# Message stage of a two-layer graph network in pairs of supersteps: half as many VectorE and ACT instructions, each twice as long

## The chip, the cores and the metric

The kernel runs on one core of one Trainium2 chip. The metric is the device time of one execution in microseconds (us), as the median of several runs.

## The reference, cut to what matters

18750 nodes with 64 features, 318750 edges, two layers. Each layer computes a gate for every edge, a degree normalisation per node, and then a message for every edge that is summed at the edge's row node:

```python
mask = jnp.clip(gate * (ZETA - GAMMA) + GAMMA, 0.0, 1.0)[:, 0]
rowsum = jax.ops.segment_sum(mask, row, num_segments=N_NODES) + EPS_DEG
d_inv_sqrt = jnp.clip(rowsum ** (-0.5), 0.0, 10.0)
vals = mask * d_inv_sqrt[row] * d_inv_sqrt[col]
msg = vals[:, None] * f2                      # f2 = x[col]
return jax.ops.segment_sum(msg, row, num_segments=N_NODES)
```

The kernel multiplies x by d_inv_sqrt first (y), so that a message is mask * y[col]; the factor of the row is applied after the sum.

## The kernel before, in words

The edges are sorted once by their column and cut into T = 156 supersteps of 2048 edges (128 lanes by CT = 16). In each layer L the stages follow one another: node scores, masks, y, **messages**, sums over rows (buckets). The change touches the message stage alone. Engines run their own instruction streams in program order and wait for one another through semaphores; a helper, steps, runs a body once, then in a hardware loop, then once more.

For superstep t the message stage does this:

- SP loads 2048 column numbers, relative to a window of 128 nodes, to all 128 partitions (crelp_d to half of the tile bcast, 512 KB, "index load") and the window's 128 rows of y, split into three bf16 parts (y_window).
- VectorE compares the index tile with the partition number: one-hots of 128 x 2048 in bf16 (col_hots, L1281).
- TensorE multiplies 16 blocks of one-hots by the three parts, 48 matmuls (spread_y, L1633). The 16 x 64 f32 values per lane take two of the six PSUM banks of psG; superstep t uses the pair of banks t % 2.
- VectorE multiplies them by the mask (scale, L1286) into scaled. ACT rounds that to bf16 (first_bf16, L835; it also writes a column of lane numbers, L836), VectorE subtracts (first_rest, L1291), ACT rounds the rest (second_bf16, L840), and VectorE subtracts again (last_part, L1295): three bf16 parts that add up to the f32 value. They stand in staged, which has four slots; superstep t uses slot t % 4.
- ACT issues the store of the slot to msg_d in DRAM (store_messages, L844, 776 KB).

The order is written out by hand. VectorE runs scale(t), last_part(t-1), one-hots(t+2), first_rest(t). ACT runs first_bf16(t), the store of t-1, second_bf16(t). SP runs the index load of t and the y window of t; the index load waits until one-hots(t-2) are made, which free its half of bcast. Each use of a staged slot begins with a wait in first_bf16 for the store that used the slot before:

```python
act.wait_ge(scaled_ready, L * T + t + 1)
wait(act, messages_stored[u], (L * T // 4 + i) * 16)
act.activation(staged[:, u, :, 0:D], scaled[:, u % 2, :, :], ACT.Copy).then_inc(first_part, 1)
```

Of the kernel before, what the change touches and what calls it, by code (L numbers as in the profile page):

```python
# [9 lines left out]
CH = 8  # L10
# [47 lines left out]
def build(nc, x, src, dst, noise, params, out):  # L58
# [21 lines left out]
    with ctx:  # L80
# [3 lines left out]
        def sem(name):  # L84
            return ctx.enter_context(nc.semaphore(name))
# [33 lines left out]
        psG = ctx.enter_context(nc.psum_tensor("psG", [P, 6, 512], f32))  # L119
        psR = ctx.enter_context(nc.psum_tensor("psR", [P, 2, 512], f32))  # L120
# [107 lines left out]
        col_one_hots = scratch[:, 0:2 * ST // 2].bitcast(bf16).rearrange("p (h e) -> p h e", h=2)  # L228
        scaled = flat_merge[:, 0:2 * CT * D].rearrange("p (h j d) -> p h j d", h=2, j=CT)
# [45 lines left out]
        lo_loaded, crel_loaded, msg_index_loaded, y_window_loaded = ([sem(f"{n}{h}") for h in range(2)] for n in ("lo_loaded", "crel_loaded", "msg_index_loaded", "y_window_loaded"))  # L275
# [59 lines left out]
        def _(sp):  # L335
# [91 lines left out]
            for L in range(2):  # L427
# [46 lines left out]
                def load_superstep(i):  # L474
                    for h in range(2):
                        t = i * 2 + h
                        wait(sp, col_hots_ready, L * T + t - 1)
                        sp.dma_start(bcast[:, 2 * h:2 * h + 2, :].rearrange("p a e -> p (a e)"),
                                     spread(crelp_d, t)).then_inc(msg_index_loaded[h], 16)
                        wait(sp, y_taken, L * T + t - 1)  # L480
                        sp.dma_start(y_window[:, h, :], y3_d[L][bass.ds(window(t * 2), P), :]).then_inc(y_window_loaded[h], 16)
                with sp.If(is_local):
                    sp.wait_ge(one_hot_ready[0], (L + 1) * T)
                    sp.wait_ge(mask_turn_kept, TURNS * (L + 1))
                    blocks = mask_d[0:whole].rearrange("(g c l) -> c g l", c=P, l=P)
# [15 lines left out]
                    steps(sp, 0, T // 2, load_superstep)  # L501
# [126 lines left out]
        def _(act):  # L628
# [70 lines left out]
            for L in range(2):  # L699
# [131 lines left out]
                def first_bf16(i, u):  # L831
                    t = i * 4 + u
                    act.wait_ge(scaled_ready, L * T + t + 1)
                    wait(act, messages_stored[u], (L * T // 4 + i) * 16)
                    act.activation(staged[:, u, :, 0:D], scaled[:, u % 2, :, :], ACT.Copy).then_inc(first_part, 1)  # L835
                    act.activation(staged[:, u, :, MW:MW + 1].bitcast(u16), row_lane[:, bass.ds(t * CT, CT)].unsqueeze(2), ACT.Copy)  # L836

                def second_bf16(t, u):
                    act.wait_ge(rest_ready, L * T + t + 1)
                    act.activation(staged[:, u, :, D:2 * D], scaled[:, u % 2, :, :], ACT.Copy).then_inc(second_part, 1)  # L840

                def store_messages(t, u):
                    act.wait_ge(third_part, L * T + t + 1)
                    act.dma_start(msg_d[bass.ds(t * TR, ST), :].rearrange("(l j) w -> l (j w)", j=CT),  # L844
                                  staged[:, u, :, :].rearrange("p j w -> p (j w)")).then_inc(messages_stored[u], 16)

                def body_local(i):
                    for u in range(4):
                        t = i * 4 + u
                        first_bf16(i, u)  # L850
                        if u > 0 or not isinstance(i, int) or i > 0:
                            store_messages(t - 1, (u - 1) % 4)
                        second_bf16(t, u)
                with act.If(is_local):
                    act.wait_ge(row_lane_loaded, 16)
                    steps(act, 0, T // 4, body_local)
                    store_messages(T - 1, 3)
                    if L == 0:
                        steps(act, 0, NG, node_beside)
# [21 lines left out]
        def _(dve):  # L881
# [240 lines left out]
            for L in range(2):  # L1122
# [154 lines left out]
                def col_hots(i, h):  # L1277
                    t = i * 2 + h
                    dve.wait_ge(msg_index_loaded[h], (L * T // 2 + i + 1) * 16)
                    wait(dve, y_taken, L * T + t - 1)  # L1280
                    dve.tensor_scalar(col_one_hots[:, h, :], bcast[:, 2 * h:2 * h + 2, :].rearrange("p a e -> p (a e)"), pid[:, 0:1], None, ALU.is_equal).then_inc(col_hots_ready, 1)  # L1281

                def scale(t, h):
                    dve.wait_ge(y_taken, L * T + t + 1)
                    wait(dve, third_part, L * T + t - 1)
                    dve.tensor_tensor(scaled[:, h, :, :], psG[:, 2 * h:2 * h + 2, :].rearrange("p a (j d) -> p (a j) d", d=D),  # L1286
                                      ga[:, bass.ds(t * CT, CT)].unsqueeze(2).to_broadcast([P, CT, D]), ALU.mult).then_inc(scaled_ready, 1)

                def first_rest(t, u):
                    dve.wait_ge(first_part, L * T + t + 1)  # L1290
                    dve.tensor_tensor(scaled[:, u % 2, :, :], scaled[:, u % 2, :, :], staged[:, u, :, 0:D], ALU.subtract).then_inc(rest_ready, 1)  # L1291

                def last_part(t, u):
                    dve.wait_ge(second_part, L * T + t + 1)
                    dve.tensor_tensor(staged[:, u, :, 2 * D:MW], scaled[:, u % 2, :, :], staged[:, u, :, D:2 * D], ALU.subtract).then_inc(third_part, 1)  # L1295

                def messages_local(i):
                    last = isinstance(i, int) and i == T // 4 - 1
                    for u in range(4):
                        t = i * 4 + u  # L1300
                        scale(t, u % 2)
                        if u > 0 or not isinstance(i, int) or i > 0:
                            last_part(t - 1, (u - 1) % 4)
                        if not last or u < 2:
                            col_hots(i * 2 + u // 2 + 1, u % 2)
                        first_rest(t, u)
# [32 lines left out]
                with dve.If(is_local):  # L1339
# [5 lines left out]
                    for h in range(2):  # L1345
                        col_hots(0, h)
                    dve.wait_ge(mask_loaded, 16 * (L + 1))
                    steps(dve, 0, T // 4, messages_local)
                    last_part(T - 1, 3)
# [71 lines left out]
        def _(pe):  # L1421
# [79 lines left out]
            for L in range(2):  # L1501
# [123 lines left out]
                def spread_y(i):  # L1625
                    for h in range(2):
                        t = i * 2 + h
                        pe.wait_ge(col_hots_ready, L * T + t + 1)
                        pe.wait_ge(y_window_loaded[h], (L * T // 2 + i + 1) * 16)
                        wait(pe, scaled_ready, L * T + t - 1)  # L1630
                        for k in range(CT):
                            for m in range(3):
                                ins = pe.matmul(psG[:, 2 * h + k // CH, k % CH * D:(k % CH + 1) * D], col_one_hots[:, h, k * P:(k + 1) * P],  # L1633
                                                y_window[:, h, m * D:(m + 1) * D], start=m == 0, stop=m == 2)
                        ins.then_inc(y_taken, 1)
# [46 lines left out]
                with pe.If(is_local):  # L1682
                    steps(pe, 0, T // 2, spread_y)
                    pe.wait_ge(scaled_ready, (L + 1) * T)
# [27 lines left out]
```

## Time and profile before

| | us |
|---|---|
| median of 3 runs | 5665.64 |
| lowest and highest | 5664.9 and 5666.88 |
| the profiled execution, its own time | 5668.84 |
| span of the profiled execution | 5667.1 |
| message stage of layer 0, first scale to last last_part | 2614.6 to 3262.2 |

The span runs from the first instruction of the program to the last; the execution's own time holds a little more around it. Views give times from the span's start. The message stage comes twice, once per layer, 156 supersteps each.

### The profile page before, as it was taken

The page shows a single profiled execution, that of the slowest core. Times are in us where ns is not written, and L with a number is a line of the kernel's source. Part 1 is how long each engine was busy: PE and PEld are TensorE (multiplying, and loading weights), DVE is VectorE, ACT ScalarE, POOL GpSimd, SP SyncE. Part 2 cuts the span into 40 slices and gives each one's busy share as a digit, 9 for nine tenths or more (in the row PEclk, how much of TensorE's full clock was granted, in tenths as well). Part 3 has the DMA queues.
Part 4 walks back from the last instruction along what each step waited for, and adds up shares of the span by engine and source line. Part 5 has one row for each costly group of instructions (what it writes and reads, how often), then busy time and mean ns, then how long its engine had stood idle before and what let it go on. Part 6 is the DMA issues. An engine that isn't in the chain of part 4 may idle for free. (4 is left out here: it accounts for less than half of the span.)

```text
span 5667.1 us, 162410 instructions
## 1 busy us (share of the span) xinstructions
PE 3982.8 (70%) x56036; PEld 3597.1 (63%) x56036; DVE 5132.4 (91%) x10844; ACT 2508.2 (44%) x5126; POOL 1165.2 (21%) x1562
## 2 busy tenths in 40 slices
PE   2777777777587888873555579978888445554777
PEld 2666666666455888872544468868888344443776
DVE  8999999999953999988999989979999799998888
ACT  2666666666423555542555511145555245554000
POOL 0000000000000333330000067723333100000776
PEclk6776777777655555556677789965555577777999
DMA  3000000000132777657999989967766589997999
GB/s 76 0 0 0 0 0 0 0 0 0 16 9 107 230 233 234 232 167 242 329 330 331 322 321 379 376 227 232 233 230 231 147 294 328 331 330 278 385 382 347
DMA packets 428684, 1120.70 MB, mean 198 GB/s; under 512 B 206962, under 2 KB 212707, under 8 KB 428023
## 3 DMA queue, kind: packets, MB, share of 16 engines
q1 hardware_dynamic: 316700, 549.97, 31.6%
q0 software_dynamic: 65856, 316.89, 14.7%
q10 hardware_dynamic: 46036, 252.74, 11.6%
q8 instruction: 42, 0.69, 0.1%
q14 instruction: 50, 0.41, 0.0%
HBM read 873.65 MB, written 279.36 MB: 203 GB/s over the span
## 5 line engine op out<-in xcount | busy, mean ns | idle before, releaser
L1633 PE MATMUL psG<-y_window,area 128*128 128x64 bf16 x14976 | 672.9, 217 | 777.8 <-DVE area L1281 619.8
L1633 PEld LDWEIGHTS psG<-y_window,area 128*128 128x128 bf16 x14976 | 629.2, 115 | 821.7 <-issue 502.3
L644 ACT ACTIVATE work<-iota,work 128x149 bf16<-128x149 f32 x2496 | 789.0, 406 | 0.0
L1452 PE MATMUL psG<-area,work 128*128 128x112 bf16 x2496 | 550.8, 390 | 336.0 <-DVE area L1004 336.0
L588 POOL DMA_INDIRECT work<-msg_d,widx x396 | 428.5, 1082 | 1657.9 <-issue 1634.8
L1452 PEld LDWEIGHTS psG<-area,work 128*128 128x128 bf16 x2496 | 357.2, 148 | 484.4 <-issue 338.5
L1445 PE MATMUL psG<-work,merge 128*128 128x148 bf16 x4992 | 548.2, 295 | 67.1 <-ACT work L644 67.1
L1445 PEld LDWEIGHTS psG<-work,merge 128*128 128x128 bf16 x4992 | 531.4, 132 | 89.9 <-issue 65.6
L840 ACT ACTIVATE work<-merge 128x1024 bf16<-128x1024 f32 x312 | 330.1, 1058 | 549.6 <-DVE merge L1291 549.6
L1666 PE MATMUL psG<-work,edge 128*128 128x192 bf16 x4752 | 443.6, 249 | 142.8 <-DVE edge L1316 141.2
L773 ACT ACTIVATE edge<-merge,npid 128x2048 bf16<-128x2048 uint16 x156 | 312.4, 2003 | 488.0 <-DMA merge<-crel_d 478.3
L1666 PEld LDWEIGHTS psG<-work,edge 128*128 128x128 bf16 x4752 | 412.4, 145 | 176.4 <-DVE edge L1316 101.1
L1316 DVE TENSOR_TENSOR edge<-y_edge,ids 128x1024 bf16<-128x1024 int16 x738 | 467.5, 688 | 8.7
L835 ACT ACTIVATE work<-merge 128x1024 bf16<-128x1024 f32 x312 | 330.1, 1058 | 198.5 <-issue 94.1
L990 DVE SCALAR_TENSOR_TENSOR work<-merge,work,psG 128x148 bf16<-128x148 f32 x1248 | 367.6, 366 | 38.8 <-ACT work L635 38.8
L990 DVE SCALAR_TENSOR_TENSOR area<-merge,work,psG 128x148 bf16<-128x148 f32 x1248 | 367.6, 366 | 23.9 <-DVE work L985 18.2
L1295 DVE TENSOR_TENSOR work<-merge,work 128x1024 bf16<-128x1024 f32 x312 | 382.4, 1226 | 2.2 <-ACT work L840 2.2
L1286 DVE TENSOR_TENSOR merge<-psG,edge 128x1024 f32<-128x1024 f32 x312 | 380.1, 1218 | 2.4 <-PE psG L1633 2.4
L1291 DVE TENSOR_TENSOR merge<-merge,work 128x1024 f32<-128x1024 f32 x312 | 380.4, 1219 | 1.0 <-ACT work L835 1.0
L547 POOL PARTITION_ALL_REDUCE wide<-wide x1 | 1.8, 1750 | 1534.5 <-DVEq L1059 1534.5
L775 ACT ACTIVATE edge<-edge 128x2048 bf16<-128x2048 bf16 x156 | 299.0, 1916 | 5.0
L565 POOL TENSOR_SCALAR area<-area 128x32 f32<-128x32 f32 x156 | 63.6, 407 | 1120.6 <-ACT area L789 1120.6
(274 smaller groups left out, 8092.8 us busy)
## 6 DMA issues: line engine op xcount, KB each, us to landing
msg_d<-work ACTq DMA_DIRECT2D x312, 776.0 KB, 4.7
area<-rlo_d SPq DMA_DIRECT2D x312, 512.0 KB, 4.2
merge<-crel_d SPq DMA_DIRECT2D x312, 512.0 KB, 5.0
area<-crelp_d SPq DMA_DIRECT2D x312, 512.0 KB, 5.8
y_window<-y_d SPq DMA_DIRECT2D x312, 48.0 KB, 3.8
y_d<-cur SPq DMA_DIRECT2D x7, 1008.0 KB, 3.8
y_d<-work SPq DMA_DIRECT2D x7, 1008.0 KB, 4.7
work<-msg_d,widx POOLq DMA_INDIRECT x396, 6.9
```

The source lines that it names most:

```text
L588: pool.indirect_dma_start(out=windows[par][:, rows.start:rows.stop, :].rearrange("p s w -> p (s w)"), out_offset=None, in_=msg_d, in_offse ...
L644: ins = act.activation(below[:, h, k, :], iota_all[:, :], ACT.Sign, bias=keyf[:, bass.ds(t * CT + k, 1)], scale=-1.0)
L835: act.activation(staged[:, u, :, 0:D], scaled[:, u % 2, :, :], ACT.Copy).then_inc(first_part, 1)
L990: ins = dve.scalar_tensor_tensor(picks[h][:, k, :], iota_half, keyf[:, bass.ds(t * CT + k, 1)], psG[:, h, 0:HB], ALU.is_equal, ALU.mult, a ...
L1286: dve.tensor_tensor(scaled[:, h, :, :], psG[:, 2 * h:2 * h + 2, :].rearrange("p a (j d) -> p (a j) d", d=D), ga[:, bass.ds(t * CT, CT)].un ...
L1291: dve.tensor_tensor(scaled[:, u % 2, :, :], scaled[:, u % 2, :, :], staged[:, u, :, 0:D], ALU.subtract).then_inc(rest_ready, 1)
L1295: dve.tensor_tensor(staged[:, u, :, 2 * D:MW], scaled[:, u % 2, :, :], staged[:, u, :, D:2 * D], ALU.subtract).then_inc(third_part, 1)
L1316: dve.tensor_tensor(q_one_hots[s][:, g, :, :], iota_rows, ids[:, s, g * WIN:(g + 1) * WIN].unsqueeze(1).to_broadcast([P, P, WIN]), ALU.is_ ...
L1445: ins = pe.matmul(psG[:, h, 0:HB], sides[:, s, :], below[:, h, k, s:s + HB], start=s == 0 and k == 0, stop=s == 1 and k == CT - 1)
L1452: ins = pe.matmul(psG[:, 2 + h, 0:RECS * CT], place[:, h, :, k], spread_rec[:, h, :, :, k], start=k == 0, stop=k == CT - 1)
L1633: ins = pe.matmul(psG[:, 2 * h + k // CH, k % CH * D:(k % CH + 1) * D], col_one_hots[:, h, k * P:(k + 1) * P], y_window[:, h, m * D:(m + 1 ...
L1666: ins = pe.matmul(psG[:, slot_, 0:MW], q_one_hots[slot_][:, r // WIN, :, r % WIN], windows[slot_][:, r, 0:MW], start=r == 0, stop=r == WG ...
```

## The change

The stage works on pairs of supersteps, n = 0 to 77 per layer. One VectorE or ACT instruction does a step for both supersteps of a pair, on 2048 f32 values per lane instead of 1024 (4096 one-hots instead of 2048). A pair takes four PSUM banks; since two pairs alternate, psG and psR become views of one PSUM tensor ps of eight banks, and the stage uses all of them. There are two sets of one-hots (scratch and a piece of edge), two sets of scaled (merge and a piece of edge) and four y windows. bcast and staged keep their size: bcast now holds one pair, staged two pairs. The order on each engine is that of before with pairs in the place of supersteps; one-hots are made two pairs ahead.

```diff
-        y_window = sb("y_window", [P, 2, MW], bf16)
+        y_window = sb("y_window", [P, 4, MW], bf16)
...
-                def load_superstep(i):
-                    for h in range(2):
-                        t = i * 2 + h
-                        wait(sp, col_hots_ready, L * T + t - 1)
-                        sp.dma_start(bcast[:, 2 * h:2 * h + 2, :].rearrange("p a e -> p (a e)"),
-                                     spread(crelp_d, t)).then_inc(msg_index_loaded[h], 16)
-                        wait(sp, y_taken, L * T + t - 1)
-                        sp.dma_start(y_window[:, h, :], y3_d[L][bass.ds(window(t * 2), P), :]).then_inc(y_window_loaded[h], 16)
+                def load_pairs(i):
+                    for v in range(2):
+                        n = i * 2 + v
+                        wait(sp, col_hots_ready, L * TP + n)
+                        for h in range(2):
+                            sp.dma_start(bcast[:, 2 * h:2 * h + 2, :].rearrange("p a e -> p (a e)"),
+                                         spread(crelp_d, n * 2 + h)).then_inc(msg_index_loaded[h], 16)
+                        wait(sp, y_taken, L * TP + n - 1)
+                        for h in range(2):
+                            sp.dma_start(y_window[:, 2 * v + h, :], y3_d[L][bass.ds(window(n * 4 + 2 * h), P), :]).then_inc(y_window_loaded[v], 16)
...
-                    wait(act, messages_stored[u], (L * T // 4 + i) * 16)
-                    act.activation(staged[:, u, :, 0:D], scaled[:, u % 2, :, :], ACT.Copy).then_inc(first_part, 1)
...
+                    for u in range(2 * v, 2 * v + 2):
+                        wait(act, messages_stored[u], (L * T // 4 + i) * 16)
+                    act.activation(staged[:, 2 * v:2 * v + 2, :, 0:D], scaled[v], ACT.Copy).then_inc(first_part, 1)
...
+                def store_messages(n, v):
+                    act.wait_ge(third_part, L * TP + n + 1)
+                    for h in range(2):
+                        act.dma_start(msg_d[bass.ds((n * 2 + h) * TR, ST), :].rearrange("(l j) w -> l (j w)", j=CT),
+                                      staged[:, 2 * v + h, :, :].rearrange("p j w -> p (j w)")).then_inc(messages_stored[2 * v + h], 16)
...
+                def body_local(i):
+                    for v in range(2):
+                        n = i * 2 + v
+                        first_bf16(i, v)
+                        if v > 0 or not isinstance(i, int) or i > 0:
+                            store_messages(n - 1, 1 - v)
+                        second_bf16(n, v)
...
+                def col_hots(n, v):
+                    for h in range(2):
+                        dve.wait_ge(msg_index_loaded[h], (L * TP + n + 1) * 16)
+                    wait(dve, y_taken, L * TP + n - 1)
+                    dve.tensor_scalar(col_one_hots[v].rearrange("p h e -> p (h e)"), bcast[:, :, :].rearrange("p a e -> p (a e)"), pid[:, 0:1], None, ALU.is_equal).then_inc(col_hots_ready, 1)
...
+                        scale(n, v)
+                        if v > 0 or not isinstance(i, int) or i > 0:
+                            last_part(n - 1, 1 - v)
+                        if not last:
+                            col_hots(n + 2, v)
+                        first_rest(n, v)
...
+                        wait(pe, scaled_ready, L * TP + n - 1)
+                        for h in range(2):
+                            for k in range(CT):
+                                for m in range(3):
+                                    ins = pe.matmul(ps[:, 4 * v + 2 * h + k // CH, k % CH * D:(k % CH + 1) * D], col_one_hots[v][:, h, k * P:(k + 1) * P],
+                                                    y_window[:, 2 * v + h, m * D:(m + 1) * D], start=m == 0, stop=m == 2)
```

On ACT, in the hardware loop of the message stage, one superstep of before (merge is the tile that holds scaled, work holds staged, edge the lane numbers; messages_stored0 to 3 tell of the landing of the stores of the four slots):

```order
L835 ACTIVATE work<-merge 128x16x64 [waits messages_stored0]
L836 ISA
L836 ACTIVATE work<-edge 128x16
L844 ISA [waits third_part]
L844 DMA msg_d<-work 128x3104
L840 ACTIVATE work<-merge 128x16x64 [waits rest_ready]
```

and one pair of the changed kernel at the same place:

```order
L840 ACTIVATE work<-merge 128x32x64 [waits messages_stored1,messages_stored0]
L841 ISA
L841 ACTIVATE work<-edge 128x32
L850 ISA [waits third_part]
L850 DMA msg_d<-work 128x3104
L850 ISA
L850 DMA msg_d<-work 128x3104
L845 ACTIVATE work<-merge 128x32x64 [waits rest_ready]
```

The first copy now waits for two stores, and two stores are issued behind one another. The next pair uses slots 2 and 3, the one after it slots 0 and 1 again.

On SP, in the hardware loop of the message stage, one superstep of before (area is the tile that holds bcast; TENSOR_LOAD reads the window's first node):

```order
L478 ISA [waits col_hots_ready]
L478 DMA area<-crelp_d 128x2048
L421 ISA [waits y_taken]
L421 TENSOR_LOAD bases
L421 ISA x2
L481 ISA
L481 DMA y_window<-y_d 128x192
```

and one pair of the changed kernel:

```order
L481 ISA [waits col_hots_ready]
L481 DMA area<-crelp_d 128x2048
L481 ISA
L481 DMA area<-crelp_d 128x2048
L313 REGISTER_ALU
L423 ISA [waits y_taken]
L423 TENSOR_LOAD bases
L423 ISA x2
L485 ISA
L485 DMA y_window<-y_d 128x192
```

Both index loads stand behind one wait for the one-hots of the pair before; the second y window of the pair follows with a TENSOR_LOAD of its own.

## Rows read from the trace of the kernel before

**Rows 1.** The page's head: busy time, share of the span and instructions by engine.
```profile
PE 3982.8 (70%) x56036; PEld 3597.1 (63%) x56036; DVE 5132.4 (91%) x10844; ACT 2508.2 (44%) x5126; POOL 1165.2 (21%) x1562
```

**Rows 2.** Stretch: busy PE, PEld, DVE, ACT, POOL (instructions), PEclk, DMA share, GB/s.
```profile
2900.00:3000.00 100.00, 51.91 (x1158) 48.50 (x1155) 100.00 (x98) 54.79 (x73) 0.00 (x0) 0.71 0.94 331
```

**Rows 3.** Groups of instructions, 2600 to 3320 us: busy, mean ns | idle before, releaser.
```profile
L1295 DVE TENSOR_TENSOR work<-merge,work 128x1024 bf16<-128x1024 f32 x156 | 191.2, 1226 | 1.1 <-ACT work L840 1.1
L1291 DVE TENSOR_TENSOR merge<-merge,work 128x1024 f32<-128x1024 f32 x156 | 190.2, 1219 | 0.5 <-ACT work L835 0.5
L1286 DVE TENSOR_TENSOR merge<-psG,edge 128x1024 f32<-128x1024 f32 x156 | 190.1, 1219 | 1.2 <-PE psG L1633 1.2
L1281 DVE TENSOR_SCALAR area<-area,pid 128x2048 bf16<-128x2048 uint16 x156 | 116.6, 748 | 4.6 <-DMA area<-crelp_d 4.6
```

**Rows 4.** Timeline of one superstep: start, duration, engine (q: sequencer), line, what.
```profile
2903.35 2.74 PE L1633 MATMUL psG<-y_window,area 128*128 128x64 bf16 x48 [2.09 <-DVE area L1281]
2903.48 0.33 SPq L478 DMA_DIRECT2D area<-crelp_d  x1
2904.35 1.22 DVE L1286 TENSOR_TENSOR merge<-psG,edge 128x1024 f32<-128x1024 f32 x1
2904.46 1.06 ACT L840 ACTIVATE work<-merge 128x1024 bf16<-128x1024 f32 x1 [1.79 <-DVE merge L1291]
2905.55 1.23 DVE L1295 TENSOR_TENSOR work<-merge,work 128x1024 bf16<-128x1024 f32 x1
2905.60 1.06 ACT L835 ACTIVATE work<-merge 128x1024 bf16<-128x1024 f32 x1
...
2906.70 0.75 DVE L1281 TENSOR_SCALAR area<-area,pid 128x2048 bf16<-128x2048 uint16 x1
...
2906.95 0.35 ACTq L844 DMA_DIRECT2D msg_d<-work  x1
2907.36 1.22 DVE L1291 TENSOR_TENSOR merge<-merge,work 128x1024 f32<-128x1024 f32 x1
...
2908.49 1.22 DVE L1286 TENSOR_TENSOR merge<-psG,edge 128x1024 f32<-128x1024 f32 x1
```

**Rows 5.** VectorE, line L946, a longer f32 operation: busy, mean ns.
```profile
L946 DVE TENSOR_TENSOR work<-edge 128x2496 f32<-128x2496 f32 x1 | 2.8, 2759 | 0.0
```

**Rows 6.** ACT, line L775, an instruction of 2048 elements: busy, mean ns.
```profile
L775 ACT ACTIVATE edge<-edge 128x2048 bf16<-128x2048 bf16 x156 | 299.0, 1916 | 5.0
```

**Rows 7.** What ended the idle time before L835, 2620 to 3280 us.
```profile
  DVE merge L1286: 5.9, 37
```

**Rows 8.** The store, line L844, 2620 to 3280 us: issue to landing.
```profile
DMA to landing us min/median/max: 3.3/4.8/6.5
```

**Rows 9.** The index load, line L478, 2620 to 3280 us: issue to landing.
```profile
DMA to landing us min/median/max: 5.1/5.9/7.0
```

**Rows 10.** DMA queues, 2904.6 to 2905.9 us: packets, MB, share (q10: stores; q1: SP's loads).
```profile
q10 hardware_dynamic: 82, 0.51, 98.3%
q1 hardware_dynamic: 31, 0.01, 3.5%
```

**Rows 11.** DMA queues, 2907.0 to 2908.0 us: packets, MB, share.
```profile
q1 hardware_dynamic: 89, 0.35, 91.7%
q10 hardware_dynamic: 1, 0.00, 0.1%
```

**Rows 12.** Timeline of the stage's first and last microseconds in layer 0.
```profile
2607.04 0.34 SPq L478 DMA_DIRECT2D area<-crelp_d  x1
...
2610.91 0.75 DVE L1281 TENSOR_SCALAR area<-area,pid 128x2048 bf16<-128x2048 uint16 x1 [3.66 <-DMA area<-crelp_d]
...
2614.57 1.22 DVE L1286 TENSOR_TENSOR merge<-psG,edge 128x1024 f32<-128x1024 f32 x1 [1.21 <-PE psG L1633]
...
3262.23 0.34 ACTq L844 DMA_DIRECT2D msg_d<-work  x1
3267.60 7.90 DVE L1352 MEMSET work<- 128x9408 f32 x1 [5.41 <-issue]
```

More of the change, by code:

```diff
@@ L118, in build @@
         dtmp = sb("dtmp", [P, CH], f32)
-        psG = ctx.enter_context(nc.psum_tensor("psG", [P, 6, 512], f32))
-        psR = ctx.enter_context(nc.psum_tensor("psR", [P, 2, 512], f32))
+        ps = ctx.enter_context(nc.psum_tensor("ps", [P, 8, 512], f32))
+        psG, psR = ps[:, 0:6, :], ps[:, 6:8, :]
         b_out = sb("b_out", [P, HI, 3], bf16)
         b_window = sb("b_window", [P, 4, 4], bf16)
-        y_window = sb("y_window", [P, 2, MW], bf16)
+        y_window = sb("y_window", [P, 4, MW], bf16)
         bases = sb("bases", [1, NS], i32)
@@ L227, in build @@
         msg = work[:, 0:4 * CH * D].rearrange("p (u k d) -> p u k d", u=4, k=CH)
-        col_one_hots = scratch[:, 0:2 * ST // 2].bitcast(bf16).rearrange("p (h e) -> p h e", h=2)
-        scaled = flat_merge[:, 0:2 * CT * D].rearrange("p (h j d) -> p h j d", h=2, j=CT)
+        col_one_hots = [t.rearrange("p (h e) -> p h e", h=2) for t in (scratch[:, 0:ST].bitcast(bf16), far[:, 0:2 * ST])]
+        scaled = [t.rearrange("p (h j d) -> p h j d", h=2, j=CT) for t in (flat_merge[:, 0:2 * CT * D], far[:, 2 * ST:4 * ST].bitcast(f32))]
         staged = work[:, 0:2 * CT * MR].bitcast(bf16).rearrange("p (h j w) -> p h j w", h=4, j=CT)
@@ L274, in build @@
         span_ready, widest_ready, local_ready, b_ready, b_stored = (sem(n) for n in ("span_ready", "widest_ready", "local_ready", "b_ready", "b_stored"))
-        lo_loaded, crel_loaded, msg_index_loaded, y_window_loaded = ([sem(f"{n}{h}") for h in range(2)] for n in ("lo_loaded", "crel_loaded", "msg_index_loaded", "y_window_loaded"))
+        lo_loaded, crel_loaded, msg_index_loaded = ([sem(f"{n}{h}") for h in range(2)] for n in ("lo_loaded", "crel_loaded", "msg_index_loaded"))
+        y_window_loaded = [sem(f"y_window_loaded{v}") for v in range(2)]
         b_window_loaded = [sem(f"b_window_loaded{s}") for s in range(4)]
@@ L838, in second_bf16 @@
[L838 to L845, printed above, removed]
@@ L847, in body_local, with first_bf16 @@
-                def body_local(i):
[L848 to L853, printed above, removed]
+                def first_bf16(i, v):
+                    n = i * 2 + v
+                    act.wait_ge(scaled_ready, L * TP + n + 1)
+                    for u in range(2 * v, 2 * v + 2):
+                        wait(act, messages_stored[u], (L * T // 4 + i) * 16)
+                    act.activation(staged[:, 2 * v:2 * v + 2, :, 0:D], scaled[v], ACT.Copy).then_inc(first_part, 1)
+                    act.activation(staged[:, 2 * v:2 * v + 2, :, MW:MW + 1].bitcast(u16), row_lane[:, bass.ds(n * 2 * CT, 2 * CT)].rearrange("l (u j) -> l u j", u=2).unsqueeze(3), ACT.Copy)
@@ new lines, in second_bf16 @@
+                def second_bf16(n, v):
+                    act.wait_ge(rest_ready, L * TP + n + 1)
+                    act.activation(staged[:, 2 * v:2 * v + 2, :, D:2 * D], scaled[v], ACT.Copy).then_inc(second_part, 1)
+                def store_messages(n, v):
[3 more added lines that the diff above has]
+                                      staged[:, 2 * v + h, :, :].rearrange("p j w -> p (j w)")).then_inc(messages_stored[2 * v + h], 16)
@@ L1283, in scale @@
[L1283 to L1291, printed above, removed]
@@ new lines, in scale, with first_rest @@
+                def scale(n, v):
+                    dve.wait_ge(y_taken, L * TP + n + 1)
+                    wait(dve, third_part, L * TP + n - 1)
+                    dve.tensor_tensor(scaled[v].rearrange("p h j d -> p (h j) d"), ps[:, 4 * v:4 * v + 4, :].rearrange("p a (j d) -> p (a j) d", d=D),
+                                      ga[:, bass.ds(n * 2 * CT, 2 * CT)].unsqueeze(2).to_broadcast([P, 2 * CT, D]), ALU.mult).then_inc(scaled_ready, 1)
+                def first_rest(n, v):
+                    dve.wait_ge(first_part, L * TP + n + 1)
+                    dve.tensor_tensor(scaled[v], scaled[v], staged[:, 2 * v:2 * v + 2, :, 0:D], ALU.subtract).then_inc(rest_ready, 1)
@@ L1297, in messages_local, with last_part @@
+                def last_part(n, v):
+                    dve.wait_ge(second_part, L * TP + n + 1)
+                    dve.tensor_tensor(staged[:, 2 * v:2 * v + 2, :, 2 * D:MW], scaled[v], staged[:, 2 * v:2 * v + 2, :, D:2 * D], ALU.subtract).then_inc(third_part, 1)
                 def messages_local(i):
                     last = isinstance(i, int) and i == T // 4 - 1
[L1299 to L1306, printed above, removed]
+                    for v in range(2):
+                        n = i * 2 + v
+                        scale(n, v)
[4 more added lines that the diff above has]
+                        first_rest(n, v)
@@ L1344, in _ @@
                     dve.memset(staged[:, :, :, MW:MR], 0.0)
-                    for h in range(2):
-                        col_hots(0, h)
+                    for v in range(2):
+                        col_hots(v, v)
                     dve.wait_ge(mask_loaded, 16 * (L + 1))
                     steps(dve, 0, T // 4, messages_local)
-                    last_part(T - 1, 3)
+                    last_part(TP - 1, 1)
                     for u in range(4):
@@ L1625, in spread_y @@
                 def spread_y(i):
[L1626 to L1634, printed above, removed]
+                    for v in range(2):
+                        n = i * 2 + v
+                        pe.wait_ge(col_hots_ready, L * TP + n + 1)
+                        pe.wait_ge(y_window_loaded[v], (L * TP + n - v + 2) * 16)
+                        wait(pe, scaled_ready, L * TP + n - 1)
[4 more added lines that the diff above has]
+                                                    y_window[:, 2 * v + h, m * D:(m + 1) * D], start=m == 0, stop=m == 2)
                         ins.then_inc(y_taken, 1)
```

21 lines of the change are left out of this document (5 added, 16 removed).

## The prediction, as it was written before the result

> **What bounds the kernel now.** I went from the whole to the stage, then to one superstep, then to its transfers. The page's head shows VectorE as the busiest engine, 91% of the span [rows 1]. That is an average over stages, so the next view is a stretch inside the stage that changes: from 2900 to 3000 us VectorE is busy for all of the 100 us, TensorE for half, ACT for 55, and the DMA engines have a share of 0.94 at 331 GB/s [rows 2]. Two things are full there, and the question is which gives way. The groups say VectorE: over a layer's stage its four operations have hardly 5 us of idle time ahead of any of them [rows 3]. The timeline shows the period: scale starts at 2904.35 and the next at 2908.49, 4.14 us for a superstep and 8.28 for two [rows 4]. Both layers have 312 supersteps, 156 pairs, 1292 us or 23% of the span. So a pair of the changed kernel that takes 0.1 us more or less than 8.28 moves the kernel by 15.6 us, and 0.2% of the kernel, about what a measurement can tell from no change, is 11.3 us.
>
> The transfers have room in time but not much in rate. A store lands 4.8 us after its issue (3.3 to 6.5) [rows 8], an index load 5.9 us after (5.1 to 7.0) [rows 9]. The store's slot is next written four supersteps later, three periods or 12 us after its issue, and in fact ACT's first copy is never held by a store, only 5.9 us in all by VectorE [rows 7]. The index load that is issued at 2903.48 is needed two supersteps after the one-hots that released it, about 7.4 us later; it lands with 1.5 us to spare.
>
> **What the change does on VectorE.** An f32 operation of 1024 elements lasts 1219 ns, one of 2496 lasts 2759 [rows 3, 5]: 1.046 ns an element, so 2048 last 1219 + 1024 x 1.046 = 2.29 us. On the engine an operation takes up its start-to-start time, which is 0.08 less: 1.14 of 1.22 us where nothing is awaited (last_part at 2905.55 to 2906.70 is 1.15, first_rest at 2907.36 to 2908.49 is 1.13) [rows 4]. Three of them take 3 x 2.21 = 6.63 us. The one-hots take 0.66 us (2906.70 to 2907.36); no row shows 4096 of them, at most they double to 1.32, at least the fixed 0.08 is saved and a little more, 1.2; I take 1.25. VectorE then needs 7.88 us for a pair instead of 8.28: 0.40 less, 62 us over 156 pairs. That is all that can be won, and only if nothing else becomes late.
>
> The Trainium skill, "VectorE: DVE Perf Modes", section on the TRN2 errata, says that an instruction with SBUF sources pays a fixed extra latency, once for a large tile and once for each of many small ones, and gives 58 cycles at 0.96 GHz; by that, four instructions fewer per pair are worth an estimated 0.24 us, 38 us in all. The rows above say 0.40, and the sum uses them.
>
> **What it does to the stores.** This is the term that I think decides. staged keeps four slots, and a pair takes two. Pair n's first copy writes the slots of pair n-2, whose stores ACT has issued just one period earlier, behind the first copy of pair n-1. The program order on ACT is thus a loop of one period: first copy, lane column, two stores issued, both landed, first copy. Its length is the time from the issue of the first store to the landing of the second, call it D, and then ACT's own part. The first copy of 2048 elements lasts about 1.9 us (an ACT instruction of 2048 shows 1916 ns [rows 6]); from a first copy to the store's issue there are now 1.35 us for a copy of 1.06, so 0.29 more [rows 4]; with 0.1 for the wake-up the part is 2.3 us. A pair can't be shorter than D + 2.3. To get the 7.88 of VectorE, D must be 5.6 us or less; to equal 8.28, 6.0.
>
> What is D? The first store alone has 3.3 us at best and 4.8 as a median [rows 8]. The second stands behind it on the same DMA engines: 0.51 MB passed in 1.3 us while stores ran [rows 10], 392 GB/s, so its 776 KB (0.795 MB) add 2.0 us: D is 5.3 to 6.8 with nothing between. Now the order of the transfers. In the stretch from 2904.6 to 2905.9 the store queue moves 0.51 MB and SP's queue 0.01 MB in 31 small packets, although the index load had been issued at 2903.48; from 2907.0 to 2908.0, when the store is through, SP's queue moves 0.35 MB and the store queue one packet [rows 4, 10, 11]. So the engines don't mix two transfers; they finish one and turn to the other queue. In the changed kernel the two stores and the two index loads are issued in the same part of each period. If the queues take turns, an index load goes between the two stores: 524 KB at 350 GB/s [rows 11], 1.5 us more. D is then 6.8 to 8.3, and the pair 9.1 to 10.6 us. I take 9.5, nearer the lower end, since the median of 4.8 already has a part of an index load ahead of the store and would count it twice.
>
> The Trainium skill, "DMA: Bandwidth & Descriptors", section Queues, rings and completion order, says that each DMA engine goes round robin between the queue rows that have work, a whole packet at a time. The trace agrees that transfers go in blocks; no stretch here has two transfers waiting on both queues, so it doesn't show the turn itself. By the rule the index load goes between the stores (9.5 us a pair), without it behind both (the second case below).
>
> **What it does to the index loads.** bcast held two supersteps, each half loaded again while the other waited; now both halves belong to one pair, and the loads for a pair are issued when the one-hots of the pair before are made. They have one period less the one-hots, 7.88 - 1.25 - 0.2 (issue) = 6.4 us, for 1 MB. With no store about, the first load of the stage is issued at 2607.04 and its one-hots start at 2610.91: 3.9 us [rows 12]. The second load of a pair adds 1.5: 5.4. That leaves 1.0 us for what stores take, and one store takes 2.0. So this loop stalls the one-hots too; at 9.5 us a pair it has 8.05, which fits 5.4 + 2.0.
>
> **What hides.** TensorE needs 2.74 us at its slower rate for a superstep [rows 4], 5.5 for a pair; it starts when one-hots two pairs ahead are made and has more than a period. The second y window comes later by one more read on SP, and TensorE's lead covers it; without that lead each late y window would cost its own microsecond.
>
> **Ends of the stage.** VectorE makes the one-hots of two pairs ahead of the first scale, now in two rounds: 2607.0 + 5.4 + 1.3 + 0.2 + 5.4 + 1.3 puts that scale at 2620.6, 6.0 us after the 2614.57 of before [rows 12]. At the end VectorE waits 5.4 us for the last store, issued at 3262.23 [rows 12]; a second store adds 2.0, the longer last copy and subtraction 0.8 + 1.1. About 10 us a layer, 20 in all.
>
> **The sum.** 156 x (9.5 - 8.28) = 190 us, and 20 for the ends: 210 more. The profiled execution took 5668.84 us, 1.7 above its span and 3.2 above the median of the runs; on the median, 5665.6 + 210 gives 5876 us.
>
> **Rivals.**
> 1. Turns as above, chance 0.55: pair 9.1 to 10.2 us, 5814 to 5986, likeliest 5876.
> 2. Both stores go first, in order of issue, 0.22. D is 5.3 to 6.8, the store loop 7.6 to 9.1. The index loads land after both stores: first issue 4.7 us into the period (scale and last_part are 4.42, then ACT), 5.3 + 3.0 later at best, at 13.0, while the one-hots want them at 7.88 + 4.42 = 12.3. A stall w moves the need twice (period and place), so w = 0.35 at best, and 1.1 with 4.8 for the first store: 8.2 to 9.1, middle 8.5. That is 156 x 0.22 + 20 = 54 more, 5720; at its lower end, 8.2, the stage itself gains 12 us and the ends cost 20: 5674, which can't be told from no change.
> 3. The other side, faster, 0.16: the transfers stay hidden. The place is ACT's first copy; it decides at D = 5.6 us. For it speaks that the fastest store took 3.3 us, and 3.3 + 2.0 = 5.3 would do, if the index loads keep out of the way; against it that the share of 0.94 leaves no stretch without a transfer ahead. Then 62 us are won and 20 paid: 5624.
> 4. Worse than turns, 0.07: both stores and both loads in one chain with the median store, 10.6 us: 156 x 2.32 + 20 = 382, 6048.
>
> Chances: faster 0.16 (case 3), within 0.2% 0.07 (the low end of case 2), slower 0.77. The range from 5615 to 5990 leaves out half of case 3 and case 4 with the edge of case 1, 0.16 together. Case 1's own range is 5814 to 5986.
>
> **What would show it.** Right: ACT's first copy waits for a store's landing in nearly each pair, VectorE's first_rest waits for that copy, and the VectorE share in the stage falls from all to about 0.83; the store's median landing rises above 6 us for the second of a pair; VectorE's f32 operations show 2.29 us and the one-hots about 1.35. A period near 7.9 with no waits at the first copy is case 3; waits only at the one-hots, for index loads, are case 2. Wrong as a whole would be a copy of 2048 elements that takes much more than 1.9 us on ACT, or a DMA that mixes the queues by the row.

## The result and the profile after

The changed kernel takes 5754.31 us (median of 4 runs, 5747.99 to 5767.25) against 5665.6, 89 us more; the ratio is estimated at 1.0159, with a 95% interval from 1.0147 to 1.0171. It is slower, as forecast, but by 89 us and not by 210. The traced execution is the longest of the four, 5767.25 us, 98.4 more than the traced one of before; what is read from its trace adds up to that, not to the 89.

The page's head of the changed kernel, which answers to [rows 1], and the two lines of its chain of work that ended last:

```profile
PE 4051.6 (70%) x56036; PEld 3689.7 (64%) x56036; DVE 5066.1 (88%) x10220; ACT 2429.8 (42%) x4658; POOL 1165.4 (20%) x1562
...
DMA 10%; DVE 6%; issue 3%; POOL 1%; SPq 1%; PE 0%; DVEq 0%; ACT 0%; POOLq 0%; ACTq 0%
DMA area<-crelp_d 8%; DVE edge L1322 2%; DVE area L1287 1%; POOL work L592 1%; DVE edge L1287 1%; DMA area<-msg_d,widx 1%; DMA work<-msg_d,widx 1%; SPq L481 1%; POOL area L592 0%; PE ps L1673 0%; DVE merge L1322 0%; DVE summed L1328 0%; DVE
```

VectorE is busy for 66 us less and the span is 98 us longer. The chain of work that ended last goes through the index loads, area<-crelp_d, with 8% of the span. The stretch that answers to [rows 2] (busy PE, PEld, DVE, ACT, POOL, then PEclk, DMA share, GB/s):

```profile
2900.00:3000.00 100.00, 54.47 (x1077) 52.90 (x1074) 89.33 (x46) 46.65 (x36) 0.00 (x0) 0.69 0.91 310
```

VectorE now idles for 11 of 100 us, and the DMA engines move less than before. The timeline of two pairs, which answers to [rows 4] (L1287 one-hots, L1292 scale, L1297 first_rest, L1301 last_part, L840 first copy, L845 second copy):

```profile
2904.80 1.29 DVE L1287 TENSOR_SCALAR edge<-area,pid 128x4096 bf16<-128x4096 uint16 x1 [2.16 <-issue]
2906.01 2.28 DVE L1297 TENSOR_TENSOR edge<-edge,work 128x2048 f32<-128x2048 f32 x1
...
2906.27 0.86 SPq L481 DMA_DIRECT2D area<-crelp_d  x2
...
2908.21 2.28 DVE L1292 TENSOR_TENSOR merge<-ps,edge 128x2048 f32<-128x2048 f32 x1
...
2910.41 2.28 DVE L1301 TENSOR_TENSOR work<-edge,work 128x2048 bf16<-128x2048 f32 x1
2910.66 1.91 ACT L840 ACTIVATE work<-merge 128x2048 bf16<-128x2048 f32 x1 [0.42 <-DVE merge L1292]
...
2912.87 0.86 ACTq L850 DMA_DIRECT2D msg_d<-work  x2
2913.10 1.29 DVE L1287 TENSOR_SCALAR area<-area,pid 128x4096 bf16<-128x4096 uint16 x1 [0.41 <-issue]
...
2914.56 1.64 SPq L481 DMA_DIRECT2D area<-crelp_d  x2
...
2919.07 1.91 ACT L840 ACTIVATE work<-edge 128x2048 bf16<-128x2048 f32 x1 [0.54 <-DMA msg_d<-work]
...
2922.28 1.29 DVE L1287 TENSOR_SCALAR edge<-area,pid 128x4096 bf16<-128x4096 uint16 x1 [1.29 <-issue]
```

Read it from one set of one-hots to the next. They end at 2906.09, their index loads are issued at 2906.27, and the next one-hots begin at 2913.10, 6.8 us later; those release loads at 2914.56, and the ones after begin at 2922.28, 7.7 us later. VectorE has a gap ahead of each ("issue": the view doesn't name a landing here). From the issues and landings in the trace, 2700 to 3200 us, the second load of a pair lands 7.2 us after the first one's issue (median; 5.8 to 9.0), and the one-hots start 0.08 us after that landing in 52 of 57 pairs. The first copy on ACT is held by a store once in this stretch: the stores are issued at 2912.87 and the copy starts at 2919.07. The waits from 2700 to 3200 us (total, times, longest) say the same:

```profile
DVE edge L1287 <- issue: 37.3, 26, 2.7
DVE area L1287 <- issue: 20.0, 20, 2.2
ACT work L840 <- DMA msg_d<-work: 15.3, 17, 1.1
```

In these 500 us, 56 pairs, VectorE loses 57 us at the one-hots, 1.0 us a pair, and ACT 15 us at the first copy. What ACT waits there hardly reaches VectorE: before first_rest, which needs the first copy, its groups from 2600 to 3400 us show 0.7 us, the other set of scaled 0.0:

```profile
L1297 DVE TENSOR_TENSOR edge<-edge,work 128x2048 f32<-128x2048 f32 x39 | 89.1, 2285 | 0.7 <-ACT work L840 0.7
L1297 DVE TENSOR_TENSOR merge<-merge,work 128x2048 f32<-128x2048 f32 x39 | 89.1, 2284 | 0.0
```

The mean period is 8.855 us in layer 0 and 8.708 in layer 1: 77 periods of each against 8.28 make 77 us. The stage as a whole, from the first index load to the clearing of work behind it, grew by 53.6 and 43.4 us, so 20 of these 97 us belong to its ends.

Where do the index loads spend 7 us? The DMA queues from 2914.4 to 2917.0 us and from 2919.0 to 2920.2 (packets, MB, share), which answer to [rows 10, 11]:

```profile
q10 hardware_dynamic: 185, 1.05, 104.8%
...
q1 hardware_dynamic: 110, 0.42, 96.7%
```

In the first stretch the two stores pass, 1.05 of their 1.59 MB in 185 packets, and not one packet of SP's queue, though its loads are issued at 2914.56. The index loads come after the second store, not after the first.

### The profile page after: what moved, and what is told of

Its sections match the earlier page's. It is cut to its first block and busy times, and to the rows that moved or that the text cites. A ratio compares the mean times of both kernels' runs of the same rounds, so it can differ in the third digit from the quotient of the medians.

```text
span 5765.4 us, 159492 instructions
## 1 busy us (share of the span) xinstructions
PE 4051.6 (70%) x56036; PEld 3689.7 (64%) x56036; DVE 5066.1 (88%) x10220; ACT 2429.8 (42%) x4658; POOL 1165.4 (20%) x1562
## 5 line engine op out<-in xcount | busy, mean ns | idle before, releaser
L1458 PE MATMUL ps<-area,work 128*128 128x112 bf16 x2496 | 551.0, 390 | 338.5 <-DVE area L1010 338.5
L1640 PE MATMUL ps<-y_window,area 128*128 128x64 bf16 x7488 | 379.9, 233 | 482.8 <-DVE area L1287 481.3
L1640 PEld LDWEIGHTS ps<-y_window,area 128*128 128x128 bf16 x7488 | 369.7, 126 | 493.0 <-issue 315.9
L1451 PE MATMUL ps<-work,merge 128*128 128x148 bf16 x4992 | 543.6, 293 | 69.9 <-ACT work L648 69.9
L1451 PEld LDWEIGHTS ps<-work,merge 128*128 128x128 bf16 x4992 | 526.7, 131 | 92.7 <-issue 66.6
L1640 PE MATMUL ps<-y_window,edge 128*128 128x64 bf16 x7488 | 366.2, 229 | 298.5 <-DVE edge L1287 298.5
L1673 PE MATMUL ps<-work,edge 128*128 128x192 bf16 x4752 | 444.4, 250 | 161.2 <-DVE edge L1322 159.7
L1673 PEld LDWEIGHTS ps<-work,edge 128*128 128x128 bf16 x4752 | 413.0, 145 | 195.0 <-DVE edge L1322 102.2
L996 DVE SCALAR_TENSOR_TENSOR work<-merge,work,ps 128x148 bf16<-128x148 f32 x1248 | 367.2, 362 | 39.6 <-ACT work L639 39.6
L996 DVE SCALAR_TENSOR_TENSOR area<-merge,work,ps 128x148 bf16<-128x148 f32 x1248 | 367.3, 362 | 23.9 <-DVE work L991 18.2
L845 ACT ACTIVATE work<-edge 128x2048 bf16<-128x2048 f32 x78 | 149.2, 1913 | 333.2 <-DVE edge L1297 333.2
L845 ACT ACTIVATE work<-merge 128x2048 bf16<-128x2048 f32 x78 | 149.2, 1913 | 309.7 <-DVE merge L1297 309.7
```

The source lines that it names most:

```text
L845: act.activation(staged[:, 2 * v:2 * v + 2, :, D:2 * D], scaled[v], ACT.Copy).then_inc(second_part, 1)
L996: ins = dve.scalar_tensor_tensor(picks[h][:, k, :], iota_half, keyf[:, bass.ds(t * CT + k, 1)], psG[:, h, 0:HB], ALU.is_equal, ALU.mult, a ...
L1451: ins = pe.matmul(psG[:, h, 0:HB], sides[:, s, :], below[:, h, k, s:s + HB], start=s == 0 and k == 0, stop=s == 1 and k == CT - 1)
L1458: ins = pe.matmul(psG[:, 2 + h, 0:RECS * CT], place[:, h, :, k], spread_rec[:, h, :, :, k], start=k == 0, stop=k == CT - 1)
L1640: ins = pe.matmul(ps[:, 4 * v + 2 * h + k // CH, k % CH * D:(k % CH + 1) * D], col_one_hots[v][:, h, k * P:(k + 1) * P], y_window[:, 2 * v ...
L1673: ins = pe.matmul(psG[:, slot_, 0:MW], q_one_hots[slot_][:, r // WIN, :, r % WIN], windows[slot_][:, r, 0:MW], start=r == 0, stop=r == WG ...
```

## The experiments

Two loops are told apart below. The index loop is: one-hots, the two index loads that they release, both landed, next one-hots. The store loop is the one that goes through the landing of a pair's two stores and the first copy that waits for it. D is, as in the prediction, the time from the issue of a pair's first store to the landing of its second; where no window is named, it is the median from 2700 to 3200 us.

**A second index buffer.** The loads of pair n wait for the one-hots of pair n-2; the buffer lies in a free part of edge.

```diff
+        index = [bcast[:, :, :].rearrange("p a e -> p (a e)"), far[:, 4 * ST:6 * ST].bitcast(u16)]
...
-                        wait(sp, col_hots_ready, L * TP + n)
+                        wait(sp, col_hots_ready, L * TP + n - 1)
...
-                            sp.dma_start(bcast[:, 2 * h:2 * h + 2, :].rearrange("p a e -> p (a e)"),
-                                         spread(crelp_d, n * 2 + h)).then_inc(msg_index_loaded[h], 16)
+                            sp.dma_start(index[v][:, h * ST:(h + 1) * ST],
+                                         spread(crelp_d, n * 2 + h)).then_inc(msg_index_loaded[v], 16)
...
-                    dve.tensor_scalar(col_one_hots[v].rearrange("p h e -> p (h e)"), bcast[:, :, :].rearrange("p a e -> p (a e)"), pid[:, 0:1], None, ALU.is_equal).then_inc(col_hots_ready, 1)
+                    dve.tensor_scalar(col_one_hots[v].rearrange("p h e -> p (h e)"), index[v], pid[:, 0:1], None, ALU.is_equal).then_inc(col_hots_ready, 1)
```

> The changed kernel with a second buffer for the indices of a pair, so that the index loads of pair n wait for the one-hots of pair n-2 instead of n-1. Index theory (the one-hots, the two index loads they release and the next one-hots form a loop of one period; second landing 7.2 us after the first issue plus 1.5 us makes the 8.9 us a pair): the loop has two periods now, the next bound is the store loop (second store lands 6.0 us after the first issue, plus 2.2) at 8.2 to 8.3 us a pair, 156 x 0.6 = about 95 us less, 5660 us. Store theory (the loop of first copy, stores and first copy sets the period, the waits at the one-hots only follow): no change, 5754 us within 10. Full engines (the 16 DMA engines are nearly always busy, and any wait that goes comes back elsewhere): about 8.6 us a pair, 5710 us.

Measured: 5767.72 us (median of 4 runs that lie far apart, 5672.66 to 5860.95), a ratio of 1.0179 to before (1.013 to 1.0228). Against the changed kernel the four lie from 82 us less to 107 more, so whether this edit alone helps isn't decided. The trace is of the 5672.66 us run, with 8.19 and 8.24 us a pair. In it the waits at the one-hots are gone, and from 2700 to 3200 us the first copy has this one:

```profile
ACT work L841 <- DMA msg_d<-work: 116.6, 61, 2.9
```

Every pair waits for a store now; VectorE loses 22 of these 500 us. D is 7.4 us (median), not 6.0. In the traced run one loop went and the other took its place, at the 8.2 us a pair that I had expected; but that agreement is luck, since I had added 2.2 to a D of 6.0, and 7.4 + 2.2 would be 9.6. The other three runs, 5744 to 5861 us, weren't traced, and what makes them longer is open.

**Six staged slots.** The first copy of pair n waits for the stores of pair n-3; the loops of ACT and VectorE take six pairs a turn.

```diff
-        staged = work[:, 0:2 * CT * MR].bitcast(bf16).rearrange("p (h j w) -> p h j w", h=4, j=CT)
+        staged = work[:, 0:3 * CT * MR].bitcast(bf16).rearrange("p (h j w) -> p h j w", h=6, j=CT)
...
-                        wait(act, messages_stored[u], (L * T // 4 + i) * 16)
+                        wait(act, messages_stored[u], (L * TP // 3 + i * 2 + p // 3) * 16)
...
```

> The changed kernel with six staged slots instead of four, so that the first copy of pair n waits for the stores of pair n-3 instead of n-2. Index theory: no change, 5754 us within 10, the first copy's 22 us of waits for stores go and the waits at the one-hots take their place. Store theory: the loop has two periods, the pair falls to the 8.2 us or less that VectorE and the index loads leave, about 5650 us. Full engines: no change.

Measured: 5756.27 us (5756.13 to 5765.61), ratio 1.0159 (1.0142 to 1.0176): no change from the changed kernel. The first copy's waits for stores are gone, and the one-hots still wait, from 2700 to 3200 us:

```profile
DVE area L1288 <- issue: 31.7, 28, 2.0
DVE edge L1288 <- issue: 18.6, 23, 1.6
```

So the store loop, on which my prediction stood, doesn't set the period of the changed kernel.

**Both.** The two edits together.

> The changed kernel with the second index buffer and with six slots. If the two loops are the whole cause: VectorE's own 8.0 us a pair (3 x 2.2 + 1.3 to 1.4), 156 x 0.9 = 140 us less than the changed kernel, about 5615 us, and faster than the kernel before by the 40 to 50 us. Full engines: 8.3 us a pair as in the kernel before, about 5670 us, with VectorE still waiting.

Measured: 5601.36 us (5599.3 to 5603.4), ratio 0.9884 (0.9868 to 0.9901). It beats the changed kernel by 153 us and the kernel before by 65. The stretch from 2700 to 2900 us:

```profile
2700.00:2900.00 200.00, 118.46 (x2496) 115.02 (x2496) 200.00 (x103) 103.92 (x77) 0.00 (x0) 0.72 0.99 351
```

VectorE is full again, and so are the DMA engines, 0.99 at 351 GB/s. A pair takes 7.77 us. With six slots in both, the second index buffer is worth 155 us (5756.27 to 5601.36): the index loop set the period. The landings of single transfers are no shorter, stores first, index loads second (issue to landing, min, median, max):

```profile
DMA to landing us min/median/max: 3.4/5.6/8.6
...
DMA to landing us min/median/max: 4.3/7.4/9.1
```

They are longer than the medians of 4.8 and 5.9 in [rows 8, 9]; two periods of slack hide them.

**One-hots in two halves**, each waiting for its own index load and releasing it.

```diff
-                        wait(sp, col_hots_ready, L * TP + n)
                         for h in range(2):
+                            wait(sp, col_hots_ready, L * T + n * 2 + h - 1)
...
                     for h in range(2):
                         dve.wait_ge(msg_index_loaded[h], (L * TP + n + 1) * 16)
-                    wait(dve, y_taken, L * TP + n - 1)
-                    dve.tensor_scalar(col_one_hots[v].rearrange("p h e -> p (h e)"), bcast[:, :, :].rearrange("p a e -> p (a e)"), pid[:, 0:1], None, ALU.is_equal).then_inc(col_hots_ready, 1)
+                        wait(dve, y_taken, L * TP + n - 1)
+                        dve.tensor_scalar(col_one_hots[v][:, h, :], bcast[:, 2 * h:2 * h + 2, :].rearrange("p a e -> p (a e)"), pid[:, 0:1], None, ALU.is_equal).then_inc(col_hots_ready, 1)
...
```

> The changed kernel with the one-hots of a pair made by two instructions, each of which waits for its own half of the indices and releases it. Index theory: the first half's load is issued 0.7 us earlier and its one-hots need the first landing (6.0 us) and not the second (7.2), so the loop shortens by 0.6 to 1.0 us to about 8.1 us a pair, VectorE pays 0.07 to 0.1; 5650 to 5680 us. Store theory and full engines: the 0.1 us a pair is lost or nothing changes, 5754 to 5770 us.

Measured: 5774.1 us (5758.26 to 5787.47), ratio 1.0198 (1.0181 to 1.0215). My expectation missed. The loads go out closer behind the stores, the first one 1.1 us after the first store and not 2.2 (medians): they land 7.7 and 8.9 us after the first load's issue, and D is 7.4. The first copies and the one-hots both wait, but VectorE loses its 45 us at the one-hots alone, so it is still the index loop, at 8.77 us a pair. From 2700 to 3200 us:

```profile
ACT work L840 <- DMA msg_d<-work: 71.4, 34, 2.7
DVE edge L1287 <- DMA area<-crelp_d: 40.6, 54, 1.5
...
DVE area L1287 <- DMA area<-crelp_d: 4.1, 10, 0.8
```

**One-hots ahead of the last subtraction**, so that the index loads go ahead of the stores.

```diff
                         scale(n, v)
+                        if not last:
+                            col_hots(n + 2, v)
                         if v > 0 or not isinstance(i, int) or i > 0:
                             last_part(n - 1, 1 - v)
-                        if not last:
-                            col_hots(n + 2, v)
                         first_rest(n, v)
```

> The changed kernel with the one-hots of pair n+2 ahead of the last subtraction of pair n-1 on VectorE, so that the index loads are issued about 2 us ahead of the stores and not 1 to 3 us behind them. Two-loop theory (transfers run in the order in which they reach an engine; an index loop and a store loop of one period each): the index loads land in 5.4 to 5.8 us, the waits at the one-hots go; the stores now stand behind them, the second lands 7 to 7.5 us after the first issue, and the store loop makes 9.0 to 9.5 us a pair: 5780 to 5870 us, no faster than the changed kernel. Index loop alone as the cause: 7.9 us a pair, 5605 us.

Measured: 5819.66 us (5817.62 to 5821.42), ratio 1.0269 (1.0252 to 1.0286), 9.12 us a pair. The loss has moved to the store loop, as the two-loop theory had it: D is 7.9, and from 2700 to 3200 us every first copy waits for a store, VectorE's first_rest for the copy, and nothing on VectorE for an index load:

```profile
ACT work L840 <- DMA msg_d<-work: 161.4, 55, 3.9
...
DVE edge L1297 <- ACT work L840: 34.5, 27, 2.2
DVE merge L1297 <- ACT work L840: 33.1, 28, 2.1
```

The period is not D + 2.2, which would be 10.1.

**Six slots and that order.**

> Six staged slots and the one-hots ahead of the last subtraction, with the one index buffer of the changed kernel. Two-loop theory: the store loop has two periods, the index loop is 5.4 to 5.8 + 1.5 = about 7.1 us and below VectorE's 7.8, so the pair takes 7.8 to 7.9 us and the kernel 5600 to 5615 us, as with both buffers. If the second index buffer is needed whatever the order: 8.3 to 8.8 us a pair, 5680 to 5760 us.

Measured: 5744.79 us (5738.68 to 5750.15), ratio 1.0135 (1.0119 to 1.0152). A miss: I had the index loads in an empty queue. Their second landing is at 7.2 us as before. From 2904.8 to 2906.0 us, behind an issue at 2904.81, the store queue still moves the pair before's stores:

```profile
q10 hardware_dynamic: 39, 0.19, 37.3%
q1 hardware_dynamic: 66, 0.05, 29.9%
```

Here the load meets the stores of the pair before, although it goes out ahead of those of its own.

**Every second index load left out** (half of the messages take wrong rows).

> The changed kernel with the index load of every second superstep left out (its one-hots are made from what the buffer held, so half of the messages take wrong rows). Two-loop theory: the loads land with the first one, 6.0 us after the issue, the index loop falls from 8.8 to about 7.4, and the store loop or VectorE is next: 7.9 to 8.2 us a pair, 5615 to 5665 us. If the period were set by the stores alone: 8.8 us, 5754.

Measured: 5617.57 us (median of 4 runs, three of them between 5615.23 and 5619.26 and one at 6150.03), ratio 0.991 (0.989 to 0.993). With one index load a pair and the one buffer, a pair takes 7.80 us in layer 0, and VectorE is full:

```profile
2700.00:2900.00 200.00, 119.24 (x2464) 115.92 (x2465) 200.00 (x104) 103.83 (x78) 0.00 (x0) 0.72 0.83 284
```

Every first copy still waits for a store, D is 6.2, and VectorE loses nothing by it (2700 to 3200 us):

```profile
ACT work L839 <- DMA msg_d<-work: 70.8, 65, 1.1
```

**The kernel before with the index load one superstep later.**

```diff
-                        wait(sp, col_hots_ready, L * T + t - 1)
+                        wait(sp, col_hots_ready, L * T + t)
```

> The kernel before, with one condition changed: the index load of superstep t waits for the one-hots of t-1 instead of t-2, so that the index loads form a loop of one period as in the changed kernel, but with single supersteps. Index theory: one-hots 0.75 + issue 0.2 + landing 4.5 to 5.9 = 5.5 to 6.9 us a superstep instead of 4.14, 6090 to 6530 us. If the loop were hidden by other work as in the kernel before: no change, 5666 us.

Measured: 5982.57 us (5979.31 to 5983.62), ratio 1.0556 (1.0539 to 1.0574). VectorE's timeline and the landing of the index load:

```profile
2901.57 0.75 DVE L1281 TENSOR_SCALAR area<-area,pid 128x2048 bf16<-128x2048 uint16 x1 [0.92 <-DMA area<-crelp_d]
...
2906.75 0.75 DVE L1281 TENSOR_SCALAR area<-area,pid 128x2048 bf16<-128x2048 uint16 x1 [0.94 <-DMA area<-crelp_d]
...
DMA to landing us min/median/max: 3.8/4.1/4.6
```

The mean period is 5.1 us (5.18 from the first line to the second): 0.75 of one-hots, 0.3 to the issue and the next start, 4.1 of landing. The loop is the same without any pairs; it costs less than expected, since the load lands in 4.1 us (267 GB/s from 2700 to 2900 us), below the 4.5 to 5.9 that I took.

## Why the prediction was off

- **VectorE.** The f32 operations last 2.28 us (2.29 forecast). With both buffers the period is 7.77 us, where I had 7.88: the one-hots take about 1.20 (2904.80 to 2906.01 above), not 1.25, and the f32 operations 2.20 (2908.21 to 2910.41), not 2.21. The saving is 0.51 us a pair, 80 us in all; the estimate of 0.24 by the Trainium skill, "VectorE: DVE Perf Modes", section on the TRN2 errata, is half of it.
- **The step that failed** is the part on the stores, in both of its terms. The first is D: "If the queues take turns, an index load goes between the two stores ... 1.5 us more. D is then 6.8 to 8.3, and the pair 9.1 to 10.6 us. I take 9.5". In the changed kernel the loads come behind both stores, and D is 6.0 (5.4 to 6.5). The second is "A pair can't be shorter than D + 2.3". With the second index buffer D is 7.4, every first copy waits for a store, and the pair takes 8.2; with half of the index loads 6.2 and 7.8; with the other order 7.9 and 9.1. Where I had 190 us for this loop, VectorE lost 0.7 us of a layer to it, and six slots alone gave nothing. Why the sum doesn't hold is shown behind this list.
- **What stood in its place** was the index loop, in the order of transfers of my second rival, which I gave 0.22: both stores first, the index loads behind them, 8.2 to 9.1 us a pair. It measured 7.2 from issue to landing + 1.5 = 8.7, against periods of 8.86 and 8.71; the prediction's own sign for that case, waits only at the one-hots, is nearly what came. I had found this loop, but took it for the lesser one. The second index buffer takes its waits away, with six slots beside it the gain comes through, half of the index loads bring it too, and in the kernel before the same loop costs 315 us (5982.57 - 5667.42 on the same chip).
- **The turn.** The rule of the Trainium skill, "DMA: Bandwidth & Descriptors", section Queues, rings and completion order (round robin between queues, a packet at a time), was wrong as I applied it, with a transfer for a packet: 1.05 MB of stores pass in a row while loads issued at 2914.56 wait. With the second buffer and with halves, where the first index load goes out 1.2 and 1.1 us behind the first store (medians), D is 7.4 and not 6.0; but with half of the index loads it also goes out 1.2 us behind, and D is 6.2. Why the second store is late in the first two was not settled.
- **ACT and the ends.** The first copy lasts 1.91 us (1.9 forecast). The ends cost 20 us, as forecast.
- **The other side**, the faster case, was a matter of two buffers: with both, the transfers stay hidden and the 0.51 us a pair comes through.

**Why not D + 2.3.** I took the 1.35 us from a first copy to the store's issue [rows 4] for ACT's own. But the issue hangs on VectorE: before, last_part ends at 2906.78 and the store goes out at 2906.95, and in every trace the median is 0.17 to 0.19 us after that end. With the second index buffer:

```profile
2916.20 0.86 ACTq L851 DMA_DIRECT2D msg_d<-work  x2
...
2921.53 2.28 DVE L1301 TENSOR_TENSOR work<-merge,work 128x2048 bf16<-128x2048 f32 x1
...
2923.69 1.91 ACT L841 ACTIVATE work<-edge 128x2048 bf16<-128x2048 f32 x1 [2.33 <-DMA msg_d<-work]
...
2923.98 0.88 ACTq L851 DMA_DIRECT2D msg_d<-work  x2
...
2925.63 2.29 DVE L1297 TENSOR_TENSOR edge<-edge,work 128x2048 f32<-128x2048 f32 x1 [0.63 <-ACT work L841]
2927.84 2.28 DVE L1292 TENSOR_TENSOR merge<-ps,edge 128x2048 f32<-128x2048 f32 x1
...
2930.04 2.28 DVE L1301 TENSOR_TENSOR work<-edge,work 128x2048 bf16<-128x2048 f32 x1
...
2932.51 0.34 ACTq L851 DMA_DIRECT2D msg_d<-work  x1
```

The second store issued at 2916.71 lands at 2923.58, and the copy that waited for it starts at 2923.69. The next store goes out 0.29 us later, while that copy still runs. What the copy does hold up is first_rest, then scale and last_part, and with them the store that follows at 2932.51: the loop closes over two pairs, from 2916.20 to 2932.51, 16.3 us or 8.2 a pair. From the start of a first copy to the issue of its own pair's store there are 8.8 us here (median and shortest of 61 pairs) and 10.0 with the other order, where the one-hots come between. D, the 0.1 us from landing to copy and this stretch add up to two periods: with the means from 2700 to 3200 us, 7.3 + 0.1 + 9.0 makes 8.2 us a pair here and 8.1 + 0.1 + 10.0 makes 9.1 with the other order, which are the periods measured. By the same sum, as an estimate, the changed kernel's 6.0 allows 7.5, below what VectorE needs, and the D of 6.8 to 8.3 that I forecast would have made 7.9 to 8.6, not 9.1 to 10.6.

## What to carry to other kernels

When steps are made twice as long over the same buffers, count for each transfer how many periods lie between its release and its need: here the index loads and the stores both fell to one period, and one period didn't cover the landing of index loads behind stores. Then follow what a late landing holds up until it comes back to the same transfer: a wait on an engine that isn't the busy one, like ACT's first copy here, can cost nothing. Two such loops can stand behind one another: six slots alone gave nothing, the second index buffer alone between 82 us less and 107 more, both together 153 us less. A landing time that is read from a trace holds for that trace's queues; moving the loads earlier changed whom they and the stores waited behind, and gave no time.

## What had not been expected

With the DMA engines at a share of 0.94 before [rows 2] I took them for nearly full. With slack they reached 0.99 at 351 GB/s against 331, so at 0.94 the engines still had room, and what the changed kernel lacked was time between a transfer's release and its need. Nor had I expected the spread with the second index buffer alone: four runs lay between 5673 and 5861 us, while the four of the changed kernel lay within 20. That every first copy waits for a store doesn't explain it, since with the other order every copy waits too and four runs lay within 4.
